# First attention of a two-layer gated block: both score maps from one 154-column product per token tile, the softmax over the tokens done with the tokens on partitions

## The reference, cut to what matters

```python
scores    = (h Wq_c + bq_c) @ (c Wk_s + bk_s).T / 16          # tokens x 77
char2sub  = softmax(scores, over the 77) @ (c Wv_s + bv_s)
scores2   = (c Wq_s + bq_s) @ (h Wk_c + bk_c).T / 16          # 77 x tokens
sub2char  = softmax(scores2, over the 1024 tokens) @ (h Wv_c + bv_c)
sub2char  = interpolate(sub2char, 77 -> 1024 rows)
gate      = sigmoid([char2sub, sub2char] @ Wg.T + bg)
x         = x + tanh(g) * (gate * char2sub + (1 - gate) * sub2char)
```

## Time and profile before

| | before |
|---|---|
| median of 3 runs | 1033.81 us (1032.59 to 1035.3) |
| the profiled execution | 1035.02 us |
| its span in the trace | 1033.1 us |
| PE busy | 1002.7 us (97%) |
| PE weight loads busy | 823.6 us (80%) |
| DVE busy | 507.1 us (49%) |
| ACT busy | 470.3 us (46%) |
| POOL busy | 303.0 us (29%) |

### The profile page before, as it was taken

The page is one execution under the profiler, slowest core; times in us unless marked ns, Lnnn a source line. Parts: engine busy times, 40 slices in busy tenths (PEclk is TensorE's granted clock), DMA queues, the critical chain, the costliest instruction groups (busy, mean ns, idle before and its releaser), DMA issues.

```text
span 1033.1 us, 14247 instructions
## 1 busy us (share of the span) xinstructions
PE 1002.7 (97%) x5190; PEld 823.6 (80%) x5190; DVE 507.1 (49%) x1374; ACT 470.3 (46%) x866; POOL 303.0 (29%) x428
## 2 busy tenths in 40 slices
PE   7999999899999998999999999999999999999997
PEld 4778777678789886887899887887888788788886
DVE  5477768886432554754233553451345355234311
ACT  1344544556434444445545454355344535533432
POOL 0005653411620513467100442311144222112111
PEclk9999999999999999999999999999999999999999
DMA  9920005703375444474665465353446535445441
GB/s 342 379 87 1 2 25 179 249 4 120 123 264 180 147 140 138 127 223 159 211 223 199 153 194 163 102 176 109 136 138 190 158 113 164 120 125 156 145 147 44
DMA packets 43548, 156.36 MB, mean 151 GB/s; under 512 B 6379, under 2 KB 6763, under 8 KB 42578
## 3 DMA queue, kind: packets, MB, share of 16 engines
q0 software_dynamic: 29952, 104.88, 33.0%
q1 hardware_dynamic: 10410, 39.19, 11.2%
q10 hardware_dynamic: 3112, 11.33, 2.8%
HBM read 136.49 MB, written 27.26 MB: 159 GB/s over the span
## 4 chain that ended last, share of the span: by engine, by line
PE 81%; DVE 7%; ACT 4%; POOL 3%; issue 3%; DMA 2%; DVEq 0%; POOLq 0%; ACTq 0%
PE psum L1130 54%; PE psum L1024 2%; PE psum L920 2%; POOL slots L2444 1%; PE psum L1210 1%; PE psum L1212 1%; PE psum L1211 1%; PE psum L778 1%; PE psum L1185 1%; PE psum L802 1%; PE psum L816 1%; PE psum L930 1%; PE psum L1050 1%; PE psum L1032 1%; PE psum L832 1%
## 5 line engine op out<-in xcount | busy, mean ns | idle before, releaser
L2428 POOL DMA_DIRECT2D mlp_pieces<-in_mlp x176 | 96.3, 553 | 441.9 <-PE psum L1130 439.2
L1130 PE MATMUL psum<-hidden_a_high,mlp_pieces 128*128 128x512 f32 x512 | 203.3, 397 | 0.0
L1130 PE MATMUL psum<-hidden_b_high,mlp_pieces 128*128 128x512 f32 x512 | 202.7, 396 | 0.1
L1130 PE MATMUL psum<-hidden_a_low,mlp_pieces 128*128 128x512 f32 x512 | 199.7, 390 | 0.0
L1130 PE MATMUL psum<-hidden_b_low,mlp_pieces 128*128 128x512 f32 x512 | 199.5, 390 | 0.0
L2263 DVE TENSOR_TENSOR hidden_a_low<-hidden_a,hidden_a_high 128x512 fp32r<-128x512 f32 x128 | 88.0, 688 | 166.3 <-ACT hidden_a_high L1613 164.6
L2263 DVE TENSOR_TENSOR hidden_b_low<-hidden_b,hidden_b_high 128x512 fp32r<-128x512 f32 x64 | 44.3, 692 | 173.5 <-ACT hidden_b_high L1613 154.2
L1630 ACT ACTIVATE hidden_a<-psum,mlp_scales 128x512 f32<-128x512 f32 x64 | 44.1, 689 | 154.8 <-PE psum L1130 148.4
L1130 PEld LDWEIGHTS psum<-hidden_a_high,mlp_pieces 128*128 128x128 f32 x512 | 96.2, 188 | 22.3 <-DVE hidden_a_low L2263 1.8
L1130 PEld LDWEIGHTS psum<-hidden_b_high,mlp_pieces 128*128 128x128 f32 x512 | 96.2, 188 | 20.8 <-issue 0.8
L1130 PEld LDWEIGHTS psum<-hidden_a_low,mlp_pieces 128*128 128x128 f32 x512 | 96.2, 188 | 20.1 <-issue 1.0
(11 more groups left out here) (294 smaller groups left out, 1802.6 us busy)
## 6 DMA issues: line engine op xcount, KB each, us to landing
mlp_pieces<-in_mlp POOLq DMA_DIRECT2D x176, 512.0 KB
mlp_piece_to_examine<-in_mlp SPq DMA_DIRECT2D x17, 512.0 KB, 4.3
yrows<-expert_rows ACTq DMA_DIRECT2D x16, 512.0 KB, 3.4
slot_rows<-slots SPq DMA_DIRECT2D x14, 512.0 KB, 4.6
slots<-in_zeros SPq DMA_DIRECT2D x1, 5120.0 KB, 46.4
x_residual<-in_x SPq DMA_DIRECT2D x4, 1024.0 KB, 23.1
out<-x_residual SPq DMA_DIRECT2D x8, 512.0 KB
slots<-in_zeros SPq DMA_DIRECT2D x1, 3072.0 KB, 32.8
```

The source lines that it names most:

```text
L1130: last = mm(o, a, b, start=(k == 0 and i == 0), stop=(k == n_k - 1 and i == len(parts) - 1))
L2428: pool.dma_start(mlp_ring[:, r % RING, :], d["mlp"][r % NCHECK]).then_inc(ring_in[r % RING], 16)
```

## The change

- The maps lie side by side (`A12`), so that one product of 154 columns for each tile gives both scores, with the tokens on partitions. Eight tiles of 154 columns need three banks: `BANKS = (2, 0, 1)` stands for banks 6, 4 and 5 with 2, 3 and 3 tiles. `a_back_scores`, `a_scores` and `a_probs_back_T` go.
- The maximum over the tokens is taken over tiles first (`a_max_back`, `a_max_lane`, on VectorE), then transposed by TensorE (`a_max_T`), reduced (`a_max_all`), and spread to all partitions by a product (`a_max_rows`). VectorE adds it to the scores (`a_less_max`), ScalarE takes exponents in place (`a_exp_back`).
- The sum over the tokens is made by four additions on GpSimd (`sum_back`) and a product with a column of ones (`a_sum_back`).
- The context's projection for the second attention (`project(w1t, 0)`) moves ahead of the turns of batch 0; the order on all queues is new, and so are the places of `invert` on GpSimd.

```diff
+        BANKS = (2, 0, 1)
+        def bank_tiles(g):
+            return range(3 * g, min(3 * g + 3, JT))
...
+            def a_both_scores(c, g):
+                pe.wait_ge(xT_r, (c + 1) * JT)
+                if c == 0:
+                    pe.wait_ge(map_v, 6)
+                elif g == 2:
+                    pe.wait_ge(t2_v, c)
                 else:
+                    pe.wait_ge(p1t_v, 2 * c - 1 + g)
+                    pe.wait_ge(p1l_v, 2 * c - 1 + g)
+                tiles = bank_tiles(g)
+                n = len(tiles)
+                mm(ps[:, 4 + g, 0:n * 2 * L], oner[:],
+                   c12[:, c].rearrange("p n c -> p (n c)").unsqueeze(1).broadcast_to([2, n, 2 * L]),
+                   start=True, stop=False)
+                for i, j in enumerate(tiles):
+                    for k in range(KC):
+                        last = mm(ps[:, 4 + g, i * 2 * L:(i + 1) * 2 * L], xnT[:, k, j * P:(j + 1) * P],
+                                  A12[:, k, c].rearrange("p n c -> p (n c)"),
+                                  start=False, stop=(i == n - 1 and k == KC - 1))
+                last.then_inc(s1b_ps, 1)
...
+                pe.transpose(ps[0:L, 7, 0:P], mxl[:], ident[:]).then_inc(mt_ps, 1)
...
+                mm(ps[:, 7, P:P + L], nm2[:].broadcast_to([L, P]), ident[0:L, 0:L], start=True, stop=True
+                   ).then_inc(mb_ps, 1)
...
+            def a_sum_back(c):
+                pe.wait_ge(sb2_r, c + 1)
+                mm(ps[0:L, 7, 2 * P:2 * P + 1], s1b[:], onec[:], start=True, stop=True).then_inc(rs_ps, 1)
...
             for c in range(1, B):
-                a_back_scores(c)
-                a_scores(c, 0)
+                for g in BANKS[:2]:
+                    a_both_scores(c, g)
                 a_sum(c - 1, 0)
-                a_scores(c, 1)
+                a_both_scores(c, BANKS[2])
                 a_sum(c - 1, 1)
-                a_probs_back_T(c)
+                a_max_T(c)
                 a_sum(c - 1, 2)
+                a_max_rows(c)
+                a_sum(c - 1, 3)
                 a_pool(c, 0)
-                a_sum(c - 1, 3)
+                a_sum(c - 1, 4)
                 a_pool(c, 1)
-                a_sum(c - 1, 4)
+                a_sum(c - 1, 5)
+                a_sum_back(c)
                 if c < B - 1:
                     a_turn(c + 1, (0, 1))
```

TensorE ahead of the loop (batch 0):

```diff
+            pe.wait_ge(map_v, 4)
+            project(w1t, 0)
             a_turn(0, range(JT))
             values(0)
             values(1)
-            a_back_scores(0)
-            a_scores(0, 0)
+            for g in BANKS:
+                a_both_scores(0, g)
             values(2)
-            a_scores(0, 1)
             values(3)
-            pe.wait_ge(map_v, 4)
-            project(w1t, 0)
-            a_probs_back_T(0)
+            a_max_T(0)
+            a_max_rows(0)
             gate_product()
             expert(0)
             a_pool(0, 0)
             expert(1)
             a_pool(0, 1)
-            for e in range(2, 5):
+            for e in range(2, 4):
                 expert(e)
+            a_sum_back(0)
+            expert(4)
             a_sub2char(0)
```

VectorE and ScalarE in the loop:

```diff
+            def a_max_back(c, g):
+                dve.wait_ge(s1b_ps, 3 * c + BANKS.index(g) + 1)
+                st.mark(dve.tensor_reduce(mx3[:, g, :], both(g)[:, 1].rearrange("p j c -> p c j"), X, ALU.max))
...
+            def a_less_max(c):
+                dve.wait_ge(mb_ps, c + 1)
+                st.link(dve.tensor_copy(mxl[:], ps[:, 7, P:P + L]))
+                for i, g in enumerate(BANKS):
+                    n = len(bank_tiles(g))
+                    dve.wait_ge(e1_r, c * JT + (2, 5, JT)[i])
+                    dve.tensor_tensor(P2T[:, 3 * g:3 * g + n, :], both(g)[:, 1],
+                                      mxl[:].unsqueeze(1).broadcast_to([P, n, L]), ALU.add).then_inc(p2d_r, 1)
...
                 if c < B - 1:
                     batch_stats(c + 1, 0)
-                a_max_back(c)
-                a_max(c, 0)
+                for g in BANKS[:2]:
+                    a_max_back(c, g)
+                    a_max(c, g)
+                a_sum(c - 1, 0)
+                a_max_back(c, BANKS[2])
+                a_max_lane(c)
+                a_max(c, BANKS[2])
+                a_max_all(c)
+                a_sum(c - 1, 1)
+                a_less_max(c)
+                a_sum(c - 1, 2)
                 if c < B - 1:
                     batch_stats(c + 1, 1)
                 if c >= 2:
                     a_measure(c - 2, (6, 7))
...
                 a_inverse(c, 0)
...
                 a_inverse(c, 1)
                 a_sum(c - 1, 3)
-                a_measure(c - 1, (1,))
+                a_measure(c - 1, (0, 1))
+                a_sum(c - 1, 4)
+                a_measure(c - 1, (2,))
                 if c < B - 1:
                     a_start(c + 1, range(4))
...
-                a_sum(c - 1, 4)
+                a_sums(c)
+                a_sum(c - 1, 5)
                 a_sub2char(c)
```

```diff
             for c in range(1, B):
+                a_exp(c, BANKS[0])
+                a_exp(c, BANKS[1])
+                a_sum(c - 1, 0)
+                a_sum(c - 1, 1)
+                a_exp(c, BANKS[2])
                 a_exp_back(c)
...
                 a_sum(c - 1, 2)
```

GpSimd:

```diff
             invert(JT, JT, 4, stats_1, inv_1)
             pool.wait_ge(inv_1, 2)
 
+            def sum_back(c):
+                pool.wait_ge(p2_r, 3 * c + 3)
+                st.link(pool.tensor_tensor(s2b[:], P2T[:, 0:2, :], P2T[:, 2:4, :], ALU.add))
+                st.link(pool.tensor_tensor(s2b[:], s2b[:], P2T[:, 4:6, :], ALU.add))
+                st.link(pool.tensor_tensor(s2b[:], s2b[:], P2T[:, 6:8, :], ALU.add))
+                pool.tensor_tensor(s1b[:], s2b[:, 0, :], s2b[:, 1, :], ALU.add).then_inc(sb2_r, 1)
+
+            sum_back(0)
             for b in range(B):
-                if b + 2 < B:
-                    invert((b + 2) * JT, JT, 2 * b + 6, stats_1, inv_1)
                 for j in range(JT):
+                    if j == 3 and b + 1 < B:
+                        sum_back(b + 1)
+                    if j == 4 and b + 2 < B:
+                        invert((b + 2) * JT, JT, 2 * b + 6, stats_1, inv_1)
+                    if j == 4 and 1 <= b < B - 1:
+                        invert((b - 1) * JT + G, G, 2 * b)
```

More of the change, by code:

```diff
@@ L279, in program @@
         lgT = place("work", "logits_T", [E, GN])
-        c1row = place("work", "score_bias_rows", [2, BL], at=cursor["work"] - GN * 4)
-        cursor["work"] += GN * 4 - 1248
+        kept = cursor["work"]
+        c12f = place("work", "score_biases", [2, 2, BL], at=kept - GN * 4)
+        cursor["work"] = kept
         lg = place("work", "logits", [P, G, 2 * E])
@@ L733, in score_biases @@
             def score_biases():
[L734 to L738 removed]
+                for n, (name, src) in enumerate((("bq_c", KT), ("bk_c", QT))):
                     for k in range(KC):
[L740 removed]
+                        last = mm(ps[0:2, 6 + n, 0:BL], col(name, k).broadcast_to([P, 2]), src[:, k, :],
                                   start=(k == 0), stop=(k == KC - 1))
@@ L806, in a_scores @@
-            def a_scores(c, q):
-                if q == 0:
-                    pe.wait_ge(bias_r, c + 1)
-                if c:
-                    pe.wait_ge(p1t_v, 2 * c - 1 + q)
-                    pe.wait_ge(p1l_v, 2 * c - 1 + q)
-                mm(ps[:, 4 + q, 0:G * L], oner[:], c1rep[:], start=True, stop=False)
-                for i in range(G):
-                    j = q * G + i
-                    for k in range(KC):
-                        last = mm(ps[:, 4 + q, i * L:(i + 1) * L], xnT[:, k, j * P:(j + 1) * P],
-                                  A1[:, k, c * L:(c + 1) * L], start=False, stop=(i == G - 1 and k == KC - 1))
-                last.then_inc(s1b_ps, 1)
@@ L834, in a_pool @@
+            def a_pool(c, k):
+                for i, g in enumerate(BANKS):
+                    if k == 0:
+                        pe.wait_ge(p2_r, 3 * c + i + 1)
+                    for j in bank_tiles(g):
+                        last = mm(ps[:, 6, (4 + k) * L:(5 + k) * L], xn[:, j, k * P:(k + 1) * P], P2T[:, j, :],
+                                  start=(j == 6), stop=(j == 5))
                 last.then_inc(r2_ps, 1)
@@ L993, in _ @@
                     a_turn(c + 1, (2, 3))
-                a_sum(c - 1, 5)
+                a_sum(c - 1, 6)
                 if c < B - 1:
@@ L998, in _ @@
                     b_turn(0, 0, (2, 3))
-                a_sum(c - 1, 6)
                 if c < B - 1:
@@ L1426, in _ @@
             a_turn(0, range(JT))
+            context_projected()
             values_high(0)
             values_high(1)
-            a_exp_back(0)
             values_high(2)
             values_high(3)
-            context_projected()
-            a_exp(0, range(JT))
-            a_probs_back_T(0)
+            for g in BANKS:
+                a_exp(0, g)
+            a_exp_back(0)
             expert(0)
@@ L1905, in _ @@
```

(31 more changed lines are left out.)

160 lines of the change are left out of this document (66 added, 94 removed).

## The result

The changed kernel takes 1046.72 us (median; 1045.77 to 1048.88) where the kernel before takes 1033.2 beside it. Paired, the ratio is 1.0132, with a 95% interval of 1.0108 to 1.0157: slower by 13.5 us. The forecast had the direction, but 6.2 us of it, and its range ended 0.7 us too low. The profiled execution took 1046.3 us, with a span of 1044.5.

A forecast was written before the change was run, and what follows sets the result against it. PE was taken to bound the first attention by a small margin. The profiled 1035.02 us plus 4.0 of waits and 2.2 of clock gave 1041.2, or 1040.0 as median; forecast 1037 to 1044 (chance 0.5), 8 in 10 from 1030.5 to 1046.

The forecast's parts named there:

- The cause: `sum_back` (2.2 us) and a late `invert` on POOL delay DVE and PE; PE waits 4.4, 3.0 and 3.0 us.
- DVE's terms: DVE, each batch: 2.9 us removed, 4.3 added, 1.4 more; maxima of 231 and 154 columns at 0.40 and 0.32.
- rival (c): Strided reads at twice the time by column, 1.5 us in batches 0 to 2, clock in full: 1046.8; chance 0.13.
- PE's products: Scores on PE: 32 instructions of 154 columns at 0.13 us, 4.2 us a batch; PE saves 2.6 us a batch.
- The walk: First attention, queues followed step by step: batches 0 to 3 change by +1.8, +1.9, +2.1 and -1.75, +4.0 us by waits.
- The clock: PE slowed to 1.2 GHz behind new idle times of 4.4, 3.0 and 3.0 us: 1.5 us each, about half taken, 2.2.
- Batch 3: Last batch of the first attention, no statistics or `a_start` in DVE's queue: 26.4 in place of 28.15, 1.75 us less.
- Rival (a): Waits come but the clock holds, or POOL and DVE are quicker: 0 to +3 us, 1033.8 to 1037; chance 0.22.
- Rival (b): Faster: POOL reaches `invert` 2.5 us earlier, so `inv_1` is ready before DVE's `a_start`: -6 us, 1027.9; chance 0.15.
- The rule on the port: Two-port DVE and POOL operations exclude each other: normalisations in batches 1 and 2 cost 0 to 1.0 us more each.

The follow-up runs named there:

- e1: The changed kernel with `sum_back(0)` ahead of the `invert` of batch 1 on POOL: 1040.53 us, ratio 1.0064 to the kernel before.
- e2: The changed kernel with the `invert` for the batch after ahead of `sum_back` and tile 3 on POOL: 1041.92 us, ratio 1.0089 to the kernel before.
- e7: The kernel before with one edit, the `invert` for the batch after behind tile 3 on POOL, not ahead of tile 0: 1034.7 us, ratio 1.0053.
- e9: e7 with 8 unread identity products on PE ahead of the turns of batches 2 and 3: 1036.74 us, ratio 1.0030 to the kernel before.
- e4: The changed kernel, order kept, with unread identity products on PE filling its waits: 1041.06 us, ratio 1.0070 to the kernel before.
- e3: The changed kernel with the edits of both e1 and e2: 1038.5 us, ratio 1.0051 to the kernel before.
- e6: e5 with each product of 154 columns made as two of 77: 1036.35 us, ratio 1.0076 to the kernel before.
- e5: The changed kernel with its POOL, DVE and PE queues laid anew, arithmetic unchanged: 1025.42 us, ratio 0.9971 to the kernel before.

## Why the prediction was right or wrong

**The cause, right.** The forecast said that `sum_back` at 2.2 us and a late `invert` on POOL make DVE late, and DVE makes PE late. The trace has `sum_back` at 2.1 us in batch 0 and 2.0 in the others, PE's wait for it in batch 0 at 4.34 (4.4 forecast), and the wait for the first normalised tile of batch 1 at 2.80 (3.0), ended at +19.95 (+20.2). e1 removes the first and takes 5.0 us out of batch 0 and 0.3 and 0.1 out of batches 1 and 2; e2 removes the second and takes 2.8 and 1.0 us out of batches 1 and 2 and 0.3 out of batch 0; e7 makes the second in the kernel before. (Batch 3 is 1.7 us shorter in e1 and e2 alike; that is the clock, see below.) Those are tests by intervention, not readings.

**DVE's terms, right.** The rows of the changed kernel, by line and form (count | busy, mean ns of one | idle time):

```profile
L1811 DVE TENSOR_REDUCE max_back_of_bank<-psum 128x77 f32<-128x231 f32 x8 | 3.2, 397 | 5.8 <-PE psum L823 5.7
L1811 DVE TENSOR_REDUCE max_back_of_bank<-psum 128x77 f32<-128x154 f32 x4 | 1.2, 311 | 0.8 <-PE psum L823 0.8
```

0.40 and 0.31 us against 0.40 and 0.32 forecast from contiguous reads, and the changed kernel's own forward maxima (L1832), which read as many elements side by side in rows of 77, take 0.39 and 0.31: that the elements are strided costs at most 0.01 us. The time came out at rival (c)'s 1046.8, which is luck: its first mechanism is not there, and the half of it that is there, the clock, is larger than it had it.

**PE's products, 0.13 us each, right.** By the step they take 1.57 / 12 = 0.131 us, and the 32 of a batch 4.4 us (4.2 forecast). But what went was priced by the chain, which counts a group to its end: by the step the back scores and forward scores took 7.8 us and not 8.0. PE saves 2.3 us on the scores, 0.4 less than forecast.

**The walk, right in its waits, 2.7 us short in its sum.** The kernel before has two falls of the clock of its own in the stage, which the walk left in its costs. One is at the end of batch 3: its eight transposes took 1.99 us, those of the changed kernel 1.10, 0.9 less. The other is among the first turns of batch 0, behind a wait which the moved projection fills in the changed kernel. Timeline of PE of the kernel before:

```profile
21.53 0.76 PE L715 MATMUL psum<-identity,x_normalised 128*128 128x128 f32 x4 [0.92 <-DVE x_normalised L1703]
22.59 0.68 PE L715 MATMUL psum<-identity,x_normalised 128*128 128x128 f32 x4 [0.30 <-ACT x_normalised_T L1358]
23.57 2.29 PE L715 MATMUL psum<-identity,x_normalised 128*128 128x128 f32 x8 [0.29 <-ACT x_normalised_T L1358]
```

In e9, where the clock held there, the way from this first turn to the bias of the first forward scores is 1.3 us shorter. No kernel with the new arithmetic has that fall. If the price of the clock is taken away on both sides, what is left is 2.0 us of loss in batch 0 (1.8 forecast), 2.9 in batch 1 (1.9), 2.5 in batch 2 (2.1) and a gain of 0.7 in batch 3 (1.75): 6.7 us of waits against +4.0. Of batches 1 and 2, 0.4 each are the scores; the gain of batch 3 was for the most part a fall that did not come again. In batch 0 the wait has the forecast length, but lies from 53.3 to 57.6 us and not from 54.8 to 59.2.

**The clock, the step that failed.** It stood in the sum at 2.2 us, "about half" of three falls at 1.5. This is the term that was mis-sized. Against other runs of the same instructions it is 2.7 us in batch 0 (e1 and e4 agree), 2.05 in batch 1 (e4), 1.7 in batch 3 (below), and about 2 in batch 2, which is only read from its rows (1.8 of it in L859). That is 8.5 us, four times the term; less the 2.2 us of the two falls that went, it is 6.3, still nearly three times. With the waits' 6.7 that makes the 13.0 by which the stage ends later, where the forecast had 4.0 and 2.2. The larger share of what was missed, 4.1 of 6.8 us, is the clock's. The price of a fall isn't fixed: in e2, behind the same wait of 4.34 us, batch 0 lost 1.0 us less than in the changed kernel. Three things were wrong. Each fall costs more than 1.5 us here: the rows that were at hand showed one fall behind eight transposes, while here L859 and the products around it run at half speed. There were four falls, not three. And half was taken where in this execution each of the long idle times brought one.

**Batch 3** is the fourth, and where the forecast gain went. It takes 28.26 us, not 26.4. Its idle times ahead of L859 are 0.36 and 0.62 us in the changed kernel and in e1 alike, and the clock fell in one and held in the other. Window of the changed kernel, then the row of e1:

```profile
156.00:158.00 2.00, 2.00 (x7) 1.13 (x6) 0.00 (x0) 0.00 (x0) 1.92 (x3) 0.50 0.00 0
```

```profile
149.89 1.92 PE L859 MATMUL psum<-attention_weights,pooled_T 128*77 128x256 f32 x8 [0.62 <-DVE inv_sum_back_gated L1838]
```

From the first score product to `a_probs_T` it is 26.9 us in the one and 25.2 in the other, 1.7 us apart, about as much as the forecast gain.

**Rival (a)**, that the clock holds, is what e4 comes near by force. Its ratio is 1.0070, but two falls are left in its trace, in batch 2 and at the end of batch 3. The waits alone are 6.7 us by the traces, and e4's execution at 0.999 is 5.1 above the fastest before: the upper end of (a), 3 us, was too low as well. **Rival (b)** needed POOL to reach `invert` 2.5 us earlier than in the walk; it began it at 90.69 - 73.56 = +17.1, 0.8 us earlier than the +17.9 of the walk, and DVE still waited 1.91 us for it.

**The rule on the port** gave 0 to 1 us for each of batches 1 and 2, and the walk 0.4. The trace separates two kinds of POOL's work. The four normalisations take 2.25 us in batch 1, beside two additions of 256 columns. In batch 2 they stand beside powers of 4 columns on POOL, and there they take the time of an undisturbed group:

```profile
125.29 1.39 DVE L1715 TENSOR_SCALAR x_normalised<-x_residual,ln_mean_var,ln_rstd 128x256 f32<-128x256 f32 x4 [1.56 <-POOL ln_rstd L2418]
```

So batch 1 paid 0.9 us, and batch 2 nothing. By the Trainium skill, SBUF — State Buffer, section Who interferes with whom, the two exclude each other for a whole instruction; the trace agrees beside the additions and shows no such price beside the small powers.

**What stays open** is when the clock falls. An idle time of 1.67 us (e2) brought it down and one of 1.94 us (e7, batch 1) and one of 2.05 us (e1, batch 0) did not; the pair in batch 3 is the same in both kernels to 0.01 us. The last wait of batch 3 tells the same: it is 1.15 or 1.16 us in the three kernels with the old arithmetic and 1.53 or 1.54 in the others, and behind it the clock fell in six of the eleven traces (before, e2, e3, e4, e6, e9) and held in five. From e5 and e6:

```profile
146.01 1.10 PE L869 MATMUL psum<-identity,probs 128*77 128x128 f32 x8 [1.53 <-DVE x_T_low L1893]
```

```profile
155.61 1.99 PE L870 MATMUL psum<-identity,probs 128*77 128x128 f32 x8 [1.53 <-DVE x_T_low L1894]
```

So a difference of 1 to 2 us between two profiled executions can be one such fall and nothing of the edit. The length of the last idle time alone doesn't decide it. No run here varied what PE does ahead of an idle time and kept all else.

## What to carry to other kernels

A step that is put into or moved past others in the in-order queue of an engine off the critical path sets when the bound engine gets its input: walk that queue before counting what the bound engine saves, and put early what it waits for first. When a cost is read from one trace, look for the clock in it first. Price each new idle time of a microsecond or more on TensorE twice, once as the wait and once as the products behind it at half their speed, here 1.6 to 2.7 us for each fall, where the clock fell, which it did not each time. And judge arithmetic and order apart: the same instructions gave 1.3% more time than the kernel before in one order and 0.3 to 0.4% less in two others.

## What the hardware did that was not expected

The clock of TensorE fell to 0.50, which is 1.2 GHz, after idle times as short as the 0.36 and 0.62 us of batch 3, with a product of 0.76 us between them, and held through 2.05 us in another run; behind one and the same wait of 1.53 us it fell in some executions and held in others. In batch 1 of the changed kernel it was still at 0.50 in the window from 97 to 99 us, with PE busy throughout, and L859 took 3.67 in place of 1.89 us. A maximum that reads PSUM with a stride of a tile took 0.397 us over 231 elements, where one that reads as many in rows of 77 side by side took 0.386. And two instructions of 77 columns took 0.22 us where one of 154 took 0.13, so that putting two narrow products side by side was worth 9.6 us in the stage.
